# Row normalisation moved off GpSimd, modulation in one pass per sequence, and a new stream order, in a four-layer transformer block

## The reference, cut to what matters

```python
def _ln(x):
    mu = jnp.mean(x, axis=-1, keepdims=True)
    var = jnp.var(x, axis=-1, keepdims=True)
    return (x - mu) * jax.lax.rsqrt(var + EPS)
...
xm = _ln(x) * (1.0 + sc_sa) + sh_sa          # sc_sa, sh_sa: one vector of channels per sequence
qkv = (xm @ qkv_w + qkv_b).reshape(B, N, 3, H, HD)
```

## Time and profile before

| | us |
|---|---|
| median of 3 runs | 1741.55 |
| lowest and highest | 1740.26, 1747.91 |
| the profiled execution, its own time | 1742.82 |
| its span, first to last instruction | 1741.0 |
| PE, PEld busy | 1633.3, 1395.3 |
| DVE busy | 1427.4 |
| ACT busy | 1364.9 |
| POOL busy | 1064.4 |

### The profile page before, as it was taken

How to read it: one execution, slowest core, us unless ns; L and a number is a source line. 1 busy time by engine, 2 the same in 40 slices (tenths; PEclk the granted TensorE clock), 3 DMA queues, 4 the chain that set the end, 5 groups by cost and what they waited for, 6 DMA issues and landing times.

```text
span 1741.0 us, 74550 instructions
## 1 busy us (share of the span) xinstructions
PE 1633.3 (94%) x31141; PEld 1395.3 (80%) x31141; DVE 1427.4 (82%) x3984; ACT 1364.9 (78%) x3517; POOL 1064.4 (61%) x1655
## 2 busy tenths in 40 slices
PE   5987899999999999999999999999999999998998
PEld 4776788888878888888888888887888878877887
DVE  6877788987878888888888888888888888888765
ACT  3665788788888878887887888788788877776886
POOL 4456565666666666666665666666675665656652
PEclk8999999999999999999999999999999999999999
DMA  7000000000000000000001000000000000000000
GB/s 234 3 15 8 18 24 24 15 18 18 24 24 24 17 16 18 24 24 24 18 10 29 18 24 24 24 3 24 24 24 24 24 15 18 18 15 15 3 2 19
DMA packets 57787, 41.23 MB, mean 24 GB/s; under 512 B 13552, under 2 KB 56176, under 8 KB 57328
## 3 DMA queue, kind: packets, MB, share of 16 engines
q1 hardware_dynamic: 57456, 36.46, 7.2%
HBM read 31.99 MB, written 4.46 MB: 21 GB/s over the span
## 4 chain that ended last, share of the span: by engine, by line
PE 57%; DVE 20%; POOL 12%; ACT 5%; issue 4%; DMA 2%; SPq 1%; POOLq 0%; DVEq 0%; ACTq 0%
DVE top L1279 8%; PE half L1106 8%; PE half L982 7%; PE half L1025 6%; PE half L1010 6%; PE half L1041 4%; POOL n_rows L799 4%; PE half L859 4%; PE half L1115 4%; PE half L958 3%; PE half L1034 3%; PE half L1051 3%; PE half L962 2%; PE half L969 2%; PE half L1004 2%
## 5 line engine op out<-in xcount | busy, mean ns | idle before, releaser
L1279 DVE TENSOR_REDUCE top<-half 128x32 f32<-128x2048 f32 x160 | 365.5, 2285 | 44.9 <-PE half L982 43.2
L1460 ACT ACTIVATE pT<-half 128x512 f32<-128x512 f32 x640 | 328.8, 607 | 74.7 <-PE half L1010 73.1
L795 POOL TENSOR_TENSOR rstd<-shifted,minus_halves 128x2 f32<-128x2 f32 x256 | 185.9, 728 | 191.6 <-DVE shifted L1241 186.0
L799 POOL TENSOR_SCALAR n_rows<-x_rows,moments,rstd 128x128 f32<-128x128 f32 x256 | 211.0, 826 | 7.8
L1495 ACT ACTIVATE pT<-half,mod 128x64 f32<-128x64 f32 x896 | 195.5, 343 | 24.9 <-PE half L1106 23.3
L827 POOL TENSOR_TENSOR top<-top 128x32 f32<-128x32 f32 x160 | 40.3, 252 | 285.3 <-DVE top L1279 285.1
L1433 ACT ACTIVATE k_heads<-half,key_bias,own_head_sb 128x256 f32<-128x256 f32 x320 | 164.0, 572 | 45.9 <-PE half L962 44.4
L1444 ACT ACTIVATE v_cols<-half 64x128 f32<-64x128 f32 x640 | 175.6, 274 | 22.6 <-PE half L969 16.2
L982 PE MATMUL half<-k_heads,q_heads 32*128 32x128 f32 x5120 | 187.8, 283 | 5.8 <-DVE q_heads L1284 1.1
L1010 PE MATMUL half<-q_heads,k_heads 32*128 32x128 f32 x5120 | 184.5, 279 | 2.2 <-issue 2.2
L982 PEld LDWEIGHTS half<-k_heads,q_heads 32*128 32x128 f32 x5120 | 160.4, 188 | 32.5 <-issue 21.2
(11 more groups left out here) (149 smaller groups left out, 3847.2 us busy)
## 6 DMA issues: line engine op xcount, KB each, us to landing
gates<-gate_store SPq DMA_DIRECT2D x128, 128.0 KB, 3.0
x_rows<-x SPq DMA_DIRECT2D x32, 128.0 KB, 2.7
c_rows<-context SPq DMA_DIRECT2D x32, 128.0 KB, 2.5
out<-n_rows SPq DMA_DIRECT2D x32, 128.0 KB, 1.8
w_sb<-weights SPq DMA_DIRECT2D x1, 1856.0 KB, 7.3
w_sb<-weights SPq DMA_DIRECT2D x2, 512.0 KB, 6.5
logit_bias<-logit_store SPq DMA_DIRECT2D x64, 1.5 KB, 3.5
row_sb<-rows SPq DMA_DIRECT2D x1, 769.5 KB, 8.2
```

Of the source, the lines that this page charges most:

```text
L795: nc.gpsimd.tensor_tensor(rstd[s][:, :], shifted[s][:, :], minus_halves[:, 0, :], ALU.pow).then_inc(rstd_in[s], 1)
L799: nc.gpsimd.tensor_scalar(n_rows[s][:, 1, :], x_rows[s][:, 1, :], moments[s][:, 1, 0:1], rstd[s][:, 1:2], ALU.subtract, ALU.mult).then_inc ...
L1279: nc.vector.tensor_reduce(term[s][0], halves[HALF_OF[n]][:, :, :].rearrange("p g (c k) -> p g c k", k=SEQ), AX.X, ALU.max).then_inc(tops_r ...
L1460: nc.scalar.activation(turn_cols[s][:, g, :], halves[HALF_OF[n]][:, g, :], ACT.Exp, scale=ATT_SCALE).then_inc(scores_read, 1)
```

## The change

VectorE normalises both row tiles at `normal`. ScalarE normalises the context rows at `c_normal`, as scale times x plus bias with both from a column; the bias, minus mean times rstd, comes from two new small GpSimd operations at `c_eps`. The modulation is made by VectorE in one step of four instructions, one for each sequence (`modulate`), straight from the PSUM bank into `nT` or `kvT`; the steps `shift` and `kvshift` are gone, and `SEQUENCE` (now 4,434 digits) is another string throughout. `HALVES` is unchanged.

```diff
 def columns(how):
-    return [("normal", None), ("cols", how)] + ([("shift", how)] if isinstance(how, tuple) else [])
+    return [("normal", None), ("cols", how)]
...
 SEQUENCE = (
-    "f21022200011122220000f00f220023f01011122110f2333014f23114443330000f421002222f00010331f02202222f11110"
+    "0f41f222f102f002201020120011211001f3002125131223003f323020001f0f23f12020400030424f1032f2022321011423"
...
                     if kind == "c_eps":
...
+                        count.next(c_rstd_in[s])
+                        means = c_moments[s][:, :, 0].unsqueeze(1).broadcast_to([D, 2, 2])
+                        nc.gpsimd.tensor_tensor(c_minus[s][:, :, :], means, c_rstd[s][:, :, :], ALU.mult).then_inc(pool_own, 1)
+                        count.next(pool_own)
+                        nc.gpsimd.tensor_scalar(c_minus[s][:, :, :], c_minus[s][:, :, :], -1.0, None, ALU.mult).then_inc(c_scaled[s], 1)
...
-                    if kind == "c_normal":
-
-                        pool.wait_ge(c_rstd_in[s], round_of(n) + 1)
-                        pool.wait_ge(a_emptied, freed_by(last_read(n), FOR_SCALAR))
-                        for t in range(2):
-                            m = nc.gpsimd.tensor_scalar(cn_rows[s][:, t, :], c_rows[s][:, t, :], c_moments[s][:, t, 0:1], c_rstd[s][:, arg, t:t + 1],
-                                                        ALU.subtract, ALU.mult)
-                        m.then_inc(c_normed[s], 1)
...
-                    if kind == "normal":
-                        count.next(rstd_in[s])
-                        nc.gpsimd.tensor_scalar(n_rows[s][:, 1, :], x_rows[s][:, 1, :], moments[s][:, 1, 0:1], rstd[s][:, 1:2],
-                                                ALU.subtract, ALU.mult).then_inc(rows_normed[s], 1)
...
+                def modulate(dst, src, s, how):
+
+                    for tb in range(GROUP):
+                        m = nc.vector.tensor_scalar(dst[:, tb, :], src[:, tb * SEQ:(tb + 1) * SEQ], mod[s][:, how[0], tb:tb + 1],
+                                                    mod[s][:, how[1], tb:tb + 1], ALU.mult, ALU.add)
+                    return m
...
                     if kind == "normal":
                         count.next(rstd_in[s])
-                        nc.vector.tensor_scalar(n_rows[s][:, 0, :], x_rows[s][:, 0, :], moments[s][:, 0, 0:1], rstd[s][:, 0:1],
-                                                ALU.subtract, ALU.mult).then_inc(rows_normed[s], 1)
+                        for t in range(2):
+                            m = nc.vector.tensor_scalar(n_rows[s][:, t, :], x_rows[s][:, t, :], moments[s][:, t, 0:1], rstd[s][:, t:t + 1],
+                                                        ALU.subtract, ALU.mult)
+                        m.then_inc(rows_normed[s], 1)
...
-                        held[s] = banks.take()
-                        makes("scaled", s, nc.vector.tensor_tensor(bank4(held[s]), bank4(held[s]), over_tokens(mod[s][:, arg[0], :]), ALU.mult))
-
-                    if kind == "shift":
-                        after("scaled", s)
-                        nc.vector.tensor_tensor(nT[s][:, :, :], bank4(held[s]), over_tokens(mod[s][:, arg[1], :]), ALU.add).then_inc(v_emptied, 1)
+                        modulate(nT[s], banks.take(), s, arg).then_inc(v_emptied, 1)
...
+                    if kind == "c_normal":
+
+                        act.wait_ge(c_scaled[s], round_of(n) + 1)
+                        for t in range(2):
+                            m = nc.scalar.activation(cn_rows[s][:, t, :], c_rows[s][:, t, :], ACT.Identity,
+                                                     scale=c_rstd[s][:, arg, t:t + 1], bias=c_minus[s][:, arg, t:t + 1])
+                        m.then_inc(c_normed[s], 1)
```

110 lines of the change are left out of this document (51 added, 59 removed).

## The result

The changed kernel took 1753.29 us (median of 8 runs, 1749.99 to 1757.17) against 1742.26 before (8 runs). The ratio is 1.0072, 95% interval 1.0058 to 1.0086: slower, where 1708 was forecast and 1742 was the upper end of the range. In what follows a ratio is always to the kernel before of the same set, with its 95% interval, and times of different sets are compared by their ratios (0.001 is 1.7 us), except where medians are named. One traced execution, that of old_ctx, took 3904 us against its median of 1739.02 and is not read. VectorE's *queue time* of an operation is the distance from its start to the next start when VectorE does not wait, and *load* is busy time as the page gives it.

A forecast was written before the change was run, and what follows sets the result against it. Bound by TensorE's fixed work plus small waits, the largest for GpSimd's half of a normalisation. 1742.8 - 34 - 3 + 19 - 6 - 4 = 1715; halfway to the chain's 1700 gave 1708 us, range 1675 to 1742.

The forecast's parts named there:

- (b): Modulation on VectorE: four 64-wide instructions at 0.19 us replace two passes; +23 us of load, 3 us saved on the path.
- (c): VectorE's load: 87 us more in all, making TensorE's waits for kvT and top grow by 19 us (bounds 0 and +87).
- (a): Row normalisation: GpSimd's half of 256 goes to VectorE, cutting TensorE's waits for n_rows; 34 us saved (bounds 12 and 55).
- R3: Rival: VectorE's tensor_scalar and GpSimd's operations exclude each other at SBUF; at worst 22 us more, 1730; chance 0.10.
- under half of 55: Sign: TensorE's waits for n_rows, now VectorE's, fall under half of 55 us.
- first 50 us over 30: Sign at the start of the kernel: TensorE busy over 30 us of the first 50.
- (d): GpSimd loses row and context normalisations, gains 64 small operations: busy 750 to 803 us; gain counted with (e).
- (e): Context rows to ScalarE, at most +73 us there; GpSimd's lighter queue shortens waits for top: 6 us with (d).
- (f): Order on TensorE: 39 fewer tile-shape changes at about 0.10 us each, 4 us saved.
- The second reading by the chain: GpSimd's normalisation line has 4% of the last-ending chain, 70 us; 49 of it go, giving 1700.
- R1: Rival: VectorE becomes the bound, each added microsecond reaching the end; 1783, or 1833 with dearer 64-wide pieces; chance 0.12.
- R2: Rival: no change, since the saved normalisation waits mostly return under VectorE's name; 1737; chance 0.11.

The follow-up runs named there:

- old_ctx: Kernel before, with only the context rows moved from GpSimd to ScalarE, in the old order: 1739.02 us, ratio 0.9986.
- new_padded: new_twopass with one more VectorE operation, for which nothing waits, behind each of the 192 modulations: 1748.37 us, ratio 1.0059.
- old_normal: Kernel before, in the old order, with only the normalisation changed: VectorE does both row tiles; 1738.25 us, ratio 0.9989.
- new_gphalf: Changed kernel in its new order, with GpSimd doing row tile 1 of each normalisation again: 1795.18 us, ratio 1.0306.
- old_mod: Kernel before, in the old order, with only the modulation changed to one pass of four 64-wide instructions: 1763.03 us, ratio 1.0127.
- new_immediate: Changed kernel with the modulation multiplying by constant 1 and adding constant 0, scale and shift left out: 1702.77 us, ratio 0.98.
- new_twopass: Changed kernel in its new order, with each modulation again in two 256-wide passes, back to back: 1726.75 us, ratio 0.9915.

## Why the prediction was wrong

The forecast was 1708 and the changed kernel took 1753, 45 us more. Two steps failed: the cost of a 64-wide piece in (b), and above all the price of a microsecond of VectorE's load in (c), 0.22 where the runs show 0.46 to 0.78. A third, smaller one is in (a) and R3: which GpSimd work holds VectorE up.

**What bounds the kernel** was half right. TensorE's busy time did not change, and the small waits decide; but "VectorE has 160 us of rest in 1000" was read as cover. new_padded shows that it is none: at 88% load, two thirds to three quarters of each further microsecond reach the end.

**(a) The halves side by side.** The waits for `n_rows` fell from 55.0 to 33.8 us in old_normal, where 21 were to stay, and to 44.1 in the changed kernel, 11 saved, just under the term's lower bound; its sign "under half of 55" failed. The wait at the start went (longest 7.2 to 2.7), but the sign "first 50 us over 30" came true by the order, since old_normal has 28.61 there and new_gphalf 32.03. In time (a) was worth nothing in the old order, in the new one 41 to 44, which is over the 34 foreseen. The prediction took one figure for a quantity that depends on the order. Its load was 73 us (old_normal) to 82 (new_gphalf to the changed kernel) and not 64, since the 0.25 per piece left the stretched ones out.

**(b) Modulation: the first step that failed.** The prediction took 0.19 us for a 64-wide piece, "the middle" between 0.13 and 0.26, and got +23 us of load. Measured: 0.252, at the upper end, +49 us (old_mod). The bounds held, but the middle between them did not, and the mistake is in the row from which it started: L1171 takes one scalar from SBUF and the new pieces take two. For one scalar the middle was right, as an estimate from L1317 and L1257 shows (0.26 less 64 columns at 1 ns is 0.19). The second scalar brings it back to 0.25, by 0.06 each in new_immediate. That sum could be made from the rows of the kernel before. The "3 us saved" for the shorter path did not show either: waits for `nT` rose from 5.8 to 18.1. With both, (b) costs 22 to 30 us where the prediction had about 2 (23 x 19/87 = 5, less 3). By new_twopass (27 us) that is 25 of the 45 us by which the forecast missed. The piece's cost alone would not have done it: 49 us at the prediction's own 0.22 are 11.

**(c) VectorE's load: the second step, and the larger.** The load was 138, not 87 us. And the growth of the waits, 0.6 x 31 = 19 us for 87, is 0.22 per microsecond; the runs show 0.46 in the old order (22.5 for 48.9, old_mod against 1740.57) and 0.57 to 0.78 in the new one (new_immediate 47 for 82.6, new_twopass 0.63, new_padded 0.67 to 0.78). The sum looked at the waits for `kvT` and `top`; `nT`, and `n_rows` itself, became VectorE's waits too. The rule weighed there, twice the rate from SBUF (the Trainium skill, VectorE: DVE Perf Modes, The perf-mode tier table), was turned down because 128-wide rows from SBUF and PSUM last the same. Those rows could not decide it, since the one from SBUF takes two scalars and the one from PSUM one. With two, 128 columns from PSUM would be about 0.32 from start to start (an estimate: 0.252 for 64, and 64 more at 1 ns), and from SBUF they are 0.254: by this estimate the trace agrees with the rule. The 33 us that the prediction worked out by it were none to be had all the same, since the 0.25 of term (a) was read off the operation from SBUF itself.

**(d), (e).** GpSimd 764.2 (750 to 803 foreseen) and ScalarE 1412.8 (1410 to 1440), as predicted; the context rows alone gave 2.4 us (0.5 to 4.5), of 6.

**(f) and the order.** Counted as 39 shape changes, 4 us; the two traces have just these, 909 and 870. With the normalisation moved, the order is worth 22 to 24. What it does beyond the shapes (which work it puts under which wait) the prediction did not price.

**The second reading by the chain**, 1700, took the forecast 7 us further down. A chain's share counts how often a line was last; it doesn't say what follows next behind it. The 13 or 14 us that are then left of the 45 are in new_twopass too, 1727 against 1713 by the sum without (b) and with (c) for 64 us; the runs don't divide them among (a), (c), (d) and the order, since (a) and the order are not worth a fixed sum each.

**R3 was real and under-priced.** It was given 22 us at worst, "the heaviest GpSimd work beside it leaves by this same change", and no part of the forecast. What stretches VectorE is GpSimd's wide `lifted` above all, which stays, and twice as many normalisations meet them; the work that left, GpSimd's half of the normalisation, had hardly done so. The stretch rose from 13.7 to 51.6 us, 38 us on VectorE where R3 had 11 at worst. Taking only the columns of `lifted` away took 37.2 us of it off and gave 37 us of time; some of that may be GpSimd's shorter work itself. The page named there (the Trainium skill, SBUF — State Buffer, Who interferes with whom) has the one that comes second blocked for the whole of the other's instruction. For VectorE behind GpSimd's wide `tensor_tensor` the trace agrees (the end 79 to 86 ns after GpSimd's, 126 times); behind GpSimd's `tensor_scalar` of 128 columns it does not (82 times, median 346 ns).

**R1 and R2.** By the prediction's own signs one of them holds: the steady stretch under 960 (953.42) and VectorE's waits above 60 us (91.9). R1 had the direction. Its price, that each added microsecond lands, was too high (0.46 to 0.78 do), and VectorE isn't the bound alone: TensorE is still busy 93% of the span.

What stays open: why the normalisation's and the context rows' moves cost 7 us together in the old order, and which places of the order make the 53 us between its two signs (+31 without, -22 with the normalisation on VectorE). No run took the order apart.

## What to carry to other kernels

Where one engine is 95% busy and a second 85%, work moved to the second isn't covered by its rest: price it with a slope (microseconds of time for each of load, here 0.46 to 0.78), and measure that slope first with a padding operation that nothing waits for. When one wide operation is to become several narrow ones with scalars from memory, price each from rows that have the same number of scalars, or add what a scalar costs; a row that agrees in width alone is not its price. Before counting on a rival's cause to leave with the change, look at which single operations the long ones run beside: here it was not GpSimd's `tensor_scalar` of 0.8 us, but those that read two wide tensors. An order searched for one placement of work is worth nothing, or less, with another: test the placement and the order together.

## What the runs showed of the hardware

- VectorE's `tensor_scalar` with two scalars read from SBUF: 0.252 us from start to start at 64 columns (from PSUM) and 0.254 at 128 (from SBUF); with two constants 0.135 at 64; with one scalar and one constant 0.26 at 128 (from PSUM). A column of an operation from PSUM is about 1 ns (`tensor_tensor`, 128 and 256 columns: 291 and 424 ns), a scalar from SBUF 50 to 60 ns.
- A normalisation on VectorE (128 columns, SBUF to SBUF) that meets a GpSimd `tensor_tensor` of 128 columns or more ends 0.08 us after that one's end (changed kernel, 126 of 128; the other two so behind a small one of 32 columns); beside GpSimd's `tensor_scalar` of 128 columns (kernel before, 82 times, median 346 ns) and its power of two columns (changed kernel, 45 times, 342 ns) it isn't held to that one's end. A modulation that reads PSUM isn't held up (108 pieces, mean 332 ns). GpSimd's `tensor_tensor` takes 739 ns at 256 columns and 462 to 467 at 128, and splitting it shortens what VectorE waits.
- ScalarE: 128 columns with two scalars 502 ns, against 572 at 256 (another line, from PSUM).
